# Setting the first token group's steps among the expert blocks to other blocks, and its row sums from GpSimd to VectorE

## What is computed

```
x = x + tanh(g_xattn[0]) * cross_attention(layernorm(x), ctx)
x = x + tanh(g_ffn[0])   * mixture_of_experts(layernorm(x))     # 16 experts, 2 picked per row; + its input
x = x + tanh(g_xattn[1]) * (layernorm(x) @ W1.T + mean(ctx) @ W2.T + b)
x = x + tanh(g_ffn[1])   * ternary_ffn(layernorm(x))            # 256 -> 1024 -> 1024 -> 1024 -> 256
```

## Time and profile before

| what | us |
|---|---|
| median of 3 runs | 495.71 (495.24 to 496.42) |
| the profiled execution's own time | 495.56 |
| its span | 493.1 |
| TensorE busy in the span | 473.1 (96%) |
| TensorE weight loads busy | 407.6 (83%) |
| VectorE busy | 314.3 (64%) |
| ScalarE busy | 217.5 (44%) |
| GpSimd busy | 148.1 (30%) |

### The profile page before, as it was taken

One profiled execution on the slowest core, in us unless ns is written; L12 is line 12 of the kernel. 1 busy time (PEld: TensorE's weight loads), 2 busy tenths in 40 slices (PEclk: granted clock), 3 DMA queues, 4 the chain that ended last, 5 costly groups with the idle time before them and its releaser, 6 DMA issues.

```text
span 493.1 us, 7864 instructions
## 1 busy us (share of the span) xinstructions
PE 473.1 (96%) x2754; PEld 407.6 (83%) x2754; DVE 314.3 (64%) x850; ACT 217.5 (44%) x444; POOL 148.1 (30%) x154
## 2 busy tenths in 40 slices
PE   8979989989898999999999999999999999999996
PEld 7868879989796788888878888987888898888886
DVE  4988979958575775575468647356964735554523
ACT  4679937765575955313362212245121124512110
POOL 1877677777812412010531201062120101000000
PEclk9999999998999999999999999999999999999998
DMA  8977535997526684311311310041121002022001
GB/s 287 370 269 253 168 95 165 310 287 220 175 89 194 229 264 157 86 43 45 117 55 43 92 58 2 0 129 48 59 85 44 1 1 85 23 64 85 23 1 50
DMA packets 34481, 58.82 MB, mean 119 GB/s; under 512 B 4545, under 2 KB 18369, under 8 KB 34370
## 3 DMA queue, kind: packets, MB, share of 16 engines
q1 hardware_dynamic: 29776, 47.12, 29.3%
q0 software_dynamic: 3840, 10.49, 7.4%
q10 hardware_dynamic: 818, 0.61, 0.5%
HBM read 47.85 MB, written 14.42 MB: 126 GB/s over the span
## 4 chain that ended last, share of the span: by engine, by line
PE 78%; DMA 4%; POOL 3%; DVE 2%; ACT 1%; issue 1%; POOLq 0%
PE bank L2037 24%; PE bank L2038 24%; PE bank L2006 6%; PE bank L2009 6%; PE bank L2070 3%; PE bank L2069 3%; PE bank L1612 3%; PE bank L1614 3%; PE bank L1613 3%; POOL xg_new L661 1%; PE bank L1849 1%; DMA xg_new<-xb_dram,perm 1%; DMA y_first<-ys_dram,slots 1%; PE bank L1852 1%; DMA xg<-xb_dram,perm 1%
## 5 line engine op out<-in xcount | busy, mean ns | idle before, releaser
L1586 ACT ACTIVATE sg<-bank,colv 128x512 f32<-128x512 f32 x64 | 44.1, 690 | 175.5 <-PE bank L2038 175.5
L2037 PE MATMUL bank<-Ah,Wr 128*128 128x512 f32 x256 | 100.1, 391 | 0.0
L2037 PE MATMUL bank<-Bh,Wr 128*128 128x512 f32 x256 | 99.9, 390 | 0.0
L2038 PE MATMUL bank<-Al,Wr 128*128 128x512 f32 x256 | 99.7, 389 | 0.0
L2038 PE MATMUL bank<-Bl,Wr 128*128 128x512 f32 x256 | 99.7, 389 | 0.0
L2037 PEld LDWEIGHTS bank<-Ah,Wr 128*128 128x128 f32 x256 | 48.0, 188 | 11.1 <-DVE Al L1299 0.6
L2037 PEld LDWEIGHTS bank<-Bh,Wr 128*128 128x128 f32 x256 | 48.1, 188 | 9.8
L2038 PEld LDWEIGHTS bank<-Bl,Wr 128*128 128x128 f32 x256 | 48.1, 188 | 9.8
L2038 PEld LDWEIGHTS bank<-Al,Wr 128*128 128x128 f32 x256 | 48.1, 188 | 9.7
L1312 DVE CAST Ah<-sg 128x512 fp32r<-128x512 f32 x32 | 13.6, 424 | 59.7 <-ACT sg L1586 59.7
L1612 PE MATMUL bank<-EL,turned 128*128 (+1 forms) x133 | 41.9, 315 | 0.3 <-ACT yb L1518 0.3
(11 more groups left out here) (298 smaller groups left out, 1021.9 us busy)
## 6 DMA issues: line engine op xcount, KB each, us to landing
Wraw<-panels SPq DMA_DIRECT2D x44, 256.0 KB, 4.1
stage<-panels SPq DMA_DIRECT2D x44, 256.0 KB, 2.6
ES<-experts SPq DMA_DIRECT2D x16, 384.0 KB, 5.9
ys_dram<-yb SPq DMA_DIRECT2D x47, 128.0 KB
ys_dram<-x SPq DMA_DIRECT2D x1, 1920.0 KB, 8.0
X<-x SPq DMA_DIRECT2D x3, 512.0 KB, 7.1
xb_dram<-xb SPq DMA_DIRECT2D x3, 512.0 KB, 4.5
out<-outb SPq DMA_DIRECT2D x3, 512.0 KB, 3.3
```

Of the source, the lines that this page charges most:

```text
L1586: eng.activation(sg[:, (8 * layer + m) % 3, :], bank[m % 4][:, :], ACT.Gelu, scale=colv[:, c + m:c + m + 1]).then_inc(f_act[m], 1)
L2037: mm(bank[m % 4][:, :], Wr[:, base:base + P], h[0][:, k, :], start=k == 0, stop=False)
L2038: ins = mm(bank[m % 4][:, :], Wr[:, base:base + P], h[1][:, k, :], start=False, stop=k == FK - 1 and not general)
```

## The change

The tables of block numbers get other values. `add_row_half` moves from POOL's loop to DVE's, directly behind `low_half`, with a wait for `crow`; `ROW_AT` goes. `statistics3_half` runs in the iteration of `x3_half` instead of one later. Transposes and their ScalarE half now share a block number (33 and 39; 44 and 46).

```
-ROOT2_AT, ROW_AT, ROOT3_AT = (40, 46), (41, 46), (46, 46)
-ADD_AT, STAT_AT = (25, 28, 31, 36), (26, 29, 33, 37)
-TURN3_AT, HIGH3_AT, LOW3_AT, PART_AT, X3_AT = (30, 37), (31, 38), (32, 39), (33, 40), (34, 41)
-NORM_AT, TURN4_AT, HIGH4_AT, LOW4_AT = (43, 45), (44, 47), (45, 48), (46, 48)
+ROOT2_AT, ROOT3_AT = (36, 42), (41, 45)
+ADD_AT, STAT_AT = (29, 32, 35, 38), (29, 32, 35, 38)
+TURN3_AT, HIGH3_AT, LOW3_AT, PART_AT, X3_AT = (33, 39), (33, 39), (34, 40), (35, 41), (36, 42)
+NORM_AT, TURN4_AT, HIGH4_AT, LOW4_AT = (43, 44), (44, 46), (44, 46), (45, 47)
...
-RESIDUAL_AT = (12, 13, 14, 15, 27, 30, 38, 40, 44, 47)
+RESIDUAL_AT = (12, 13, 14, 15, 25, 26, 27, 28, 31, 37)
...
@@ gpsimd @@
-            def add_row_half(q):
-                ts, _ = halves(q)
-                eng.wait_ge(n_T, q + 1)
-                eng.tensor_tensor(X[:, ts, :], X[:, ts, :], crow[:, 0:1, :].to_broadcast([P, 2, D]), ALU.add).then_inc(n_row, 1)
...
-                    if i == ROW_AT[q]:
-                        add_row_half(q)
...
@@ vector @@
+            def add_row_half(q):
+                ts, _ = halves(q)
+                eng.wait_ge(n_T, q + 1)
+                eng.wait_ge(act_setup, ACT_LATE + 2)
+                eng.tensor_tensor(X[:, ts, :], X[:, ts, :], crow[:, 0:1, :].to_broadcast([P, 2, D]), ALU.add).then_inc(n_row, 1)
...
                     if i == LOW3_AT[q]:
                         low_half(q, n_h3, n_l3)
+                        add_row_half(q)
                     if i == X3_AT[q]:
                         x3_half(q)
-                    if i == X3_AT[q] + 1:
                         statistics3_half(q)
```

## The result

The changed kernel takes 509.76 us, median of 6 runs (507.25 to 512.64), against 495.04 of 6 runs of the kernel before (494.34 to 496.42): ratio 1.0296, 95% interval 1.0257 to 1.0335. It is slower, as forecast, by 14.7 us where some 8 had been forecast; 509.76 lies above the range, which ended at 507.5.

The account below looks back on a forecast made before the run. TensorE was taken as the bound, at the gathers' limit in the block stage. Last gather's landing 149.14 + 8.93 + 1.66 put the feed-forward at 159.73, 8.02 later: 495.56 + 8.02 = 503.6 us, range 498.5 to 507.5.

Parts of the forecast that it names:

- The end: Block 46's turn to the first feed-forward matmul: 8.93 us as before, plus 1.66 for lower clock behind the third stall.
- the third stall: TensorE waits 4.68 us for gather 46, held on POOL behind the last kind's second root.
- Landing of 37 and the root in front of it: Gather 37: root adds 0.63 us, issue at 120.76, landing takes 4.2, rows turned at 124.96.
- Roots in front of gathers: On POOL, waiting roots hold gathers 42, 43 and 46; TensorE stalls 1.44, 1.96 and 4.68 us.
- The loop of 7.48: Start of a TensorE iteration through VectorE's statistics and POOL's kind-3 root to the next gather's landing: 7.48 us.
- Adding the tiles later: Adds four blocks later: VectorE's wait goes, with TensorE's 2.82 us and 1.66 of clock; the gather is late next.
- Row sums on VectorE: Two sums move from POOL to VectorE at 0.68 us each, hidden; new wait for `crow` and the transposes costs nothing.
- Residuals on POOL: Four residuals run on VectorE in iterations 25 to 28, beside gather issues; POOL loses nothing.
- VectorE becomes the bound: Rival: VectorE limits iterations 34 to 36, for 1.14 us more, 504.7 us; chance 0.08.
- POOL is held by the residuals: Rival: three more residuals ahead of gather 37 block POOL for 1.7 us, 505.3 us; chance 0.04.
- Only the last root holds a gather: Rival: gathers 42 and 43 land in time, so stalls 1.44 and 1.96 go, 500.2 us; chance 0.14.
- The gathers keep up: Rival: POOL issues faster than 1.25 us, block 37 turned at 118.90, feed-forward some 7 earlier, 488.5 us; chance 0.05.

Follow-up runs that it names:

- With fillers: Changed kernel with needless identity matmuls (10, 8 and 20 calls) in TensorE's waits for gathers 37, 43 and 46: 506.8 us, ratio 1.0253.
- the first two experiments: Changed kernel with only the last kind's roots behind the last gather, 502.68 us; then with all late roots behind it, 497.04 us.
- two of the other kernels: Changed kernel with all late roots behind the last gather, 497.04 us; kernel before with its late roots one block earlier, 502.6 us.
- the first spread kernel: Changed kernel with the eight result fetches spread, roots at (42, 46) and (46, 46) and the steps behind them moved to suit: 492.34 us, ratio 0.9947.

## Why the prediction was right in kind and too small

The forecast's chain, step by step, from the turns above:

| step | forecast | measured | miss |
|---|---|---|---|
| turn of block 37 | 124.96 | 125.53 | +0.57 |
| 37 to 38 | 2.93 | 4.22 | +1.29 |
| 38 to 42 | 7.48 | 7.84 | +0.36 |
| 42 to 43 | 3.36 | 3.68 | +0.32 |
| 43 to 44 | 2.93 | 4.36 | +1.43 |
| 44 to 46 | 7.48 | 7.87 | +0.39 |
| 46 to the feed-forward, clock included | 10.59 | 11.15 | +0.56 |

Together 4.92. With 1.02 outside the span and 0.16 behind, that is the 6.1 by which the profiled 509.68 passes the forecast 503.6.

**The step that failed** is the term for the clock in *The end*: "so I add 1.66", once, for the third stall alone. The clock fell behind the waits at 37 and 43 as well, and cost 5.13 in place of 1.66, 3.47 more. In the table these are the steps 37 to 38, 43 to 44 and 46 to the feed-forward, 3.28 of the 4.92, since the forecast's 2.93, 2.93 and 8.93 without clock were 0.19 longer than the 2.88, 2.83 and 8.89 at full clock. The row to take the term from was there, and it was carried to one wait of three: the text put stalls of 1.44 and 1.96 beside a 2.82 that had cost clock, and let them pass for shorter. Of block 37 it called a wait of 6.1 "spread" and gave it no clock at all; measured, it was 2.05 at 33 and 3.17 at 37. The range missed for the same reason: its lower end dropped the clock, and its upper end never counted it three times.

**Landing of 37 and the root in front of it.** The root of kind 2 was priced at 0.63 without a wait; it waited 1.52, and gather 37 went out at 122.20 instead of 120.76. The landing, 3.2 instead of 4.2, gave back 1.0 of that. Two errors that nearly cancel.

**Roots in front of gathers.** Right in place and kind: POOL idle 5.18, 1.51 and 8.00, forecast as 5.0, 1.5 and 6.0. The loop of 7.48 measured 7.84 and 7.87, and most of the rest is the landing. At 46 it is 3.99 from the turn of 44 to the root, for 3.85; 0.90 to the issue, for 0.93; and 2.98 to the turn, for 2.7. At 42 it is 3.98, 0.91 and 2.95. Block 43 too was turned 3.20 behind its issue. At 42 the last releaser named is VectorE's `turned` (wait 0.90), whose iteration holds a tile's adds and statistics; the gather issued at 134.64 comes at nearly the same time, for issues from 119 on landed in 2.8 in the median, which gives 137.44. With fillers, the same block's wait of 2.16 is put down to the gather. Which of the two was later by a tenth is left open.

**Adding the tiles later.** Right: the wait in `row_added` went, and TensorE's wait for gathers took its place, in the changed kernel and alone (2.88 for 2.82, or for the 2.20 of the kernel that it was built on).

**Row sums on VectorE.** Right at 0.68 each and hidden; a gather's issue that began at 123.53, while the first of them ran, took 1.26 instead of 0.95 (1.40 and 1.13 in the kernels of the first two experiments). The 1.1 they save is real by themselves, ratio 0.9945; in the changed kernel it lies in front of a gather and is worth nothing there. "I cost it at nothing" was wrong outside the span. Every run of every kernel with the sums on VectorE has 3.0 to 3.6 us there, the one with nothing but the sums moved included; every run of the kernel before and of that with its late roots one block earlier has 2.0 to 2.6. So the 1.02 of the profiled execution came with this part of the change. What in it takes the time no run here tells.

**Residuals on POOL.** Costed at nothing, and the trace agrees: the issues at 105.04, 106.29, 107.55 and 108.79 took 0.94 or 0.95 with a residual beside each, and the residuals, which began at 105.37, 106.77, 108.17 and 109.57, took 0.41, 0.59, 0.43 and 0.40. By the Trainium skill's page "SBUF — State Buffer", section "Who interferes with whom", where an instruction of VectorE in a two-port mode and one of GpSimd meet, the one that starts first holds the ports that both use, and the other blocks fully. Each issue began first, so by that rule VectorE would be the one to wait, and not POOL; that also holds for the row that the prediction read as speaking against it. The trace agrees in so far as POOL lost nothing and one residual was stretched, by 0.18; a full block it doesn't show, for the residual at 105.37 took its 0.41 inside an issue.

**The rivals** fell as weighed. With the late roots taken away the kernel stands at 497.04, not to be told from the kernel before, so "VectorE becomes the bound" and "POOL is held by the residuals" don't explain the loss; the longest waits that are left there are for gathers. "Only the last root holds a gather" falls by the waits at 43, in the changed kernel and with that root alone. "The gathers keep up" falls by the 3.17 at 37.

Open: what makes up the 1.02 outside the span, why the landings behind a root were 2.95 to 3.20 where 2.7 had been read, and which of gather and VectorE came last at 42.

## What to carry to other kernels

In a queue that runs in order, ask of every step that waits what is queued behind it: a root of 0.7 us was free behind the last gather and made TensorE wait 3.9 and 4.9 us in front of it. A wait that is removed from one engine has to be followed to the next one that is late; here it turned into one of the same length. And where the trace shows that a pause of the bounding engine was followed by a lower clock, put that price on each pause of the forecast that is as long, as the upper end at least.

## What the runs showed of the hardware

The clock's price came behind shorter waits than expected, and not behind every one. In the changed kernel waits of 2.05, 3.17, 2.10 and 4.92 each had a stretch of 0.50 to 0.62 behind them (the one at block 33: 0.56 from 114.51 to 117.50), while the 0.90 at block 42 left it at 1.00. In two of the other kernels waits of 2.25 and 1.94 at block 37 were followed by 0.50 (123.72 to 127.00) and 0.61 (125.90 to 130.24). But the 2.18 of the first spread kernel, and the 3.18 at block 43 of the kernel with only the last kind's roots moved, were followed by 1.00. The stretch behind the 2.18, in the table's columns:

```profile
120.45:123.50 3.05, 3.05 (x27) 3.05 (x28) 1.93 (x5) 1.89 (x6) 2.14 (x4) 1.00 0.77 273
```

And the one behind the 3.18, in the other kernel:

```profile
146.06:149.50 3.44, 3.44 (x30) 3.44 (x31) 0.79 (x2) 1.20 (x4) 2.19 (x3) 1.00 0.46 145
```

So a single wait of 2 to 3 us is a chance of 1.3 to 1.5 us more, not a certainty; why these two were spared no run here tells.
